# Second feed-forward of a four-layer graph network on Trainium2: work of four tiles of tokens interleaved, orders of the engines rewritten, scan stored in half the columns

## What is computed

```python
# 8 heads of 64; per graph: x is 256 tokens x 128
fx = x @ W_fx.T + b_fx;  xm = x @ W_x.T + b_x
sw = softmax((xm @ W_slice.T + b_slice) / temp)      # token -> 64 slices, per head
snorm = sw.sum(tokens)
st = einsum('bhnc,bhng->bhgc', fx, sw) / (snorm + 1e-5)   # 64 pooled tokens a graph, 512 wide
zxbcdt = st @ in_w.T                                 # z, x, B, C, dt forward and backward
dt = softplus(dt + dt_bias)
xBC = silu(causal_conv3(xBC))
y = scan(dt, exp(-dt*exp(A_log)), B, C, x)           # forward and backward over the 64 tokens
y = y + x * (x @ fcD_w.T + Dp)
yg = y * silu(z);  yg = yg * rsqrt(mean(yg**2) + 1e-5) * norm_w
ot = yg @ out_w.T
out = einsum('bhgc,bhng->bhnc', ot, sw) @ out_w.T + out_b
```

## Time and profile before

| what | value |
|---|---|
| median of three runs | 3244.88 us |
| profiled execution, from its first to its last instruction | 3243.7 us |
| TensorE busy in it | 2606.3 us, 80% |
| VectorE busy | 2274.7 us, 70% |
| ScalarE busy | 1783.4 us, 55% |
| GpSimd busy | 867.6 us, 27% |
| mean granted TensorE clock | 0.914 |
| this feed-forward | 1361 to 2071 us of the span |

### The profile page before, as it was taken

One profiled execution on the slowest core, in us unless ns is written; L12 is line 12 of the kernel. 1 busy time (PEld: TensorE's weight loads), 2 busy tenths in 40 slices (PEclk: granted clock), 3 DMA queues, 4 the chain that ended last, 5 costly groups with the idle time before them and its releaser, 6 DMA issues. The chain is left out here.

```text
span 3243.7 us, 68706 instructions
## 1 busy us (share of the span) xinstructions
PE 2606.3 (80%) x19386; PEld 2087.8 (64%) x19386; DVE 2274.7 (70%) x6679; ACT 1783.4 (55%) x5130; POOL 867.6 (27%) x863
## 2 busy tenths in 40 slices
PE   5899996992776941789999999699996888759992
PEld 4577776992675941656776777566664555549992
DVE  6777774666685656667777777499997688835555
ACT  2344434663674532755565555377774777726664
POOL 0233334663343432300000000000001155534442
PEclk9899997996887975989999999799998999969996
DMA  5111112334321213200000000000001000012225
GB/s 200 46 59 59 59 34 76 84 84 127 125 77 48 66 59 118 82 1 1 0 0 0 0 0 1 22 21 21 24 19 67 5 28 28 29 42 65 63 62 175
DMA packets 142548, 168.55 MB, mean 52 GB/s; under 512 B 19920, under 2 KB 118224, under 8 KB 141776
## 3 DMA queue, kind: packets, MB, share of 16 engines
q1 hardware_dynamic: 116688, 118.67, 12.1%
q0 software_dynamic: 21504, 44.74, 4.0%
q10 hardware_dynamic: 4224, 3.59, 0.4%
HBM read 115.87 MB, written 51.05 MB: 51 GB/s over the span
## 5 line engine op out<-in xcount | busy, mean ns | idle before, releaser
L1198 POOL DMA_INDIRECT y_rows<-ffn_e_rows_out,ffn_e_scatter_at x352 | 339.7, 965 | 385.7 <-DVE ffn_e_rows_out L1226 218.4
L1340 PE MATMUL bank<-ffn_e_xT,ffn_e_mine 128*128 128x128 f32 x3360 | 439.6, 278 | 2.2 <-ACT ffn_e_xT L1272 1.4
L1340 PEld LDWEIGHTS bank<-ffn_e_xT,ffn_e_mine 128*128 128x128 f32 x3360 | 410.4, 195 | 3.4 <-ACT ffn_e_xT L1272 2.2
L722 POOL DMA_INDIRECT sorted_rows<-ffn_rows,ffn_slot x320 | 315.5, 986 | 278.8 <-issue 266.4
L1274 ACT ACTIVATE ffn_e_mine<-constants 128x512 f32 (+1 forms) x352 | 250.2, 712 | 114.6 <-issue 65.3
L1246 DVE TENSOR_TENSOR ffn_e_hid<-ffn_e_act,bank 128x256 f32<-128x256 f32 (+1 forms) x280 | 136.1, 486 | 225.0 <-ACT ffn_e_act L1300 199.8
L1350 PE MATMUL bank<-ffn_e_mine,ffn_e_hid 128*128 128x128 f32 x1968 | 278.0, 276 | 2.6 <-DVE ffn_e_hid L1250 2.4
L2566 ACT ACTIVATE gnn_prob<-bank,gnn_low 128x256 f32<-128x256 f32 x512 | 203.5, 501 | 107.1 <-DVE gnn_low L2480 107.1
L1350 PEld LDWEIGHTS bank<-ffn_e_mine,ffn_e_hid 128*128 128x128 f32 x1968 | 247.5, 192 | 5.3 <-DVE ffn_e_hid L1250 4.8
L1300 ACT ACTIVATE ffn_e_act<-bank 128x256 f32<-128x256 f32 (+1 forms) x280 | 120.9, 432 | 106.0 <-PE bank L1340 104.9
L2480 DVE TENSOR_REDUCE gnn_low<-bank 128x2 f32<-128x512 f32 x256 | 159.0, 684 | 24.1 <-PE bank L2665 21.3
(11 more groups left out here) (505 smaller groups left out, 6583.6 us busy)
## 6 DMA issues: line engine op xcount, KB each, us to landing
g_adj<-in_adjT SPq DMA_DIRECT2D x48, 512.0 KB, 4.0
ffn_e_rows_in<-sorted_rows SPq DMA_DIRECT2D x346, 66.0 KB
ffn_c_y<-y_rows SPq DMA_DIRECT2D x80, 256.0 KB, 3.2
g_adj_rows<-in_adj SPq DMA_DIRECT2D x16, 512.0 KB, 4.3
gnn_adj<-in_adjT SPq DMA_DIRECT2D x16, 512.0 KB, 4.0
constants<-in_ffn SPq DMA_DIRECT2D x1, 6281.0 KB, 22.2
y_rows<-ffn_e_rows_out,ffn_e_scatter_at POOLq DMA_INDIRECT x352, 2.2
constants<-in_ffn SPq DMA_DIRECT2D x1, 5204.0 KB, 15.4
```

The lines of the kernel that those rows point to most:

```text
L722: eng.indirect_dma_start(c.sorted_rows, bass.IndirectOffsetOnAxis(r.slot[par][:, k, j:j + 1], 0), r.rows[par][:, j, :], None).then_inc(r.d ...
L1198: g.indirect_dma_start(c.y_rows, bass.IndirectOffsetOnAxis(scatter_at[par][:, k:k + 1], 0), rows_out[par][:, k, :], None).then_inc(scatter ...
L1340: ins = pe.matmul(chunk(part, ch), chunk(weights[:, i * HALF:(i + 1) * HALF], ch), x, start=True, stop=True)
```

## The change

`every_turn` is replaced for this stage by `staggered`, which writes turns -2 to 3 and 12 to 18 out and loops over 4 to 11. In one turn t the engines now do the logits of t+1, pooling and projections of t, scan of t-1, and outputs of t-2; X is updated for t-3. Every engine's `turn` is a new list in a new order, with the waits standing in it. To make room, sz, rsm and swT have two buffers, the projections use other banks, and `square` has a buffer of its own.

Three pieces of arithmetic are stored otherwise. Each head's scan matrix keeps only the block of the row's own graph, 64 columns instead of 128 (`own_masks`, `dt_run`, `dt_both`, `factor`, `decay`); the running sums become two 128x512 matmuls, the product with the tokens 16 matmuls of 64x64 weights. The sums over tokens ride in the unused half of the weights of the value matmuls (`value_w` has columns of ones), so L2294 is gone, and `pooled` does both graphs at once. dt is spread by VectorE alone.

```diff
+def staggered(eng, body, ahead, behind):
+
+    for t in range(-ahead, 4):
+        body(t, t % 2)
+    with eng.Fori(4, TURNS - 4, 2) as t:
+        body(t, 0)
+        body(t + 1, 1)
+    for t in range(TURNS - 4, TURNS + behind):
+        body(t, t % 2)
...
+                def turn(t, par):
+                    if on(t):
+                        after(g, g8_ready, t)
+                        after(g, xtok_ready, t)
+                        skip_term()
+                    if on(t - 1):
+                        add_bias(t - 1)
...
+                def pooled(t):
+
+                    low_half, high_half = slice(0, SL), slice(SL, P)
+                    v.tensor_scalar(sn[low_half], B[5][high_half, :], 1e-5, None, ALU.add)
+                    then(v, v.tensor_scalar(sn[high_half], B[4][low_half, :], 1e-5, None, ALU.add), stn, 2 * t + 1)
+                    then(v, v.reciprocal(sn[:], sn[:]), stn, 2 * t + 2)
...
+                def spread_dt():
+                    v.tensor_tensor(dt_run[:], dt[:].rearrange("p (d h) -> p d h", d=2)[:, :, :, None].broadcast_to([P, 2, HEADS2, SL]),
+                                    own_masks[:, :, None, :].broadcast_to([P, 2, HEADS2, SL]), ALU.mult).then_inc(dt_run_ready, 1)
...
+                def exp_dt():
+                    a.activation(e[:], m[:], ACT.Exp).then_inc(spe_ready, 1)
...
-                def pool_sums(t, g):
-                    pe.wait_ge(ph_ready, t * 2 + g + 1)
-                    mm(B[5 + 2 * g][:], ones[:], pooled_h[:, g, :], start=True, stop=True).then_inc(norm_ps, 1)
+                def pool_values():
+                    for a in range(2):
+                        for j in range(KC):
+                            cols = slice((2 * j + a) * SL, (2 * j + a + 1) * SL)
+                            ins = mm(B[5 - a][:, j * P:(j + 1) * P], value_w[:, a, j, :], pooled_h[:, :, cols], start=True, stop=True)
...
+                def running_sums():
+                    for d in range(2):
+                        ins = mm(B[3][:], masks[:, 1 - d, :], dt_run[:, d].rearrange("p h n -> p (h n)"), start=(d == 0), stop=(d == 1))
+                    ins.then_inc(D_ps, 1)
+
+                def product_y():
+                    for g in range(2):
+                        rows_ = slice(g * SL, (g + 1) * SL)
+                        for hd in range(HEADS2):
+                            cols = slice(hd * HD2, (hd + 1) * HD2)
+                            ins = mm(B[7][rows_, cols], decay[rows_, hd, :], xtok[rows_, cols], start=True, stop=True)
+                    ins.then_inc(y_ps, 1)
...
+                    if on(t + 1):
+                        after(pe, decay_ready, t - 1)
+                        lg_piece(1)
```

More of the change, by code:

```diff
@@ L46, in every_turn, with on, after @@
     body(count - 1, 1, False, True)
+def on(turn):
+    return not isinstance(turn, int) or 0 <= turn < TURNS
+def after(eng, sem, turn, each=1, nth=1):
+    if on(turn):
+        eng.wait_ge(sem, turn * each + nth)
+def staggered(eng, body, ahead, behind):
[6 more added lines that the diff above has]
+        body(t, t % 2)
 def every_four(eng, body):
@@ L1993, in pooled @@
[L1993 to L2007, removed]
+                    lg = heads(LG[k][:])
@@ L2106, in turn @@
-                    if not first:
-                        residual(t - 1)
-                    v.wait_ge(y_ps, t + 1)
-                    v.wait_ge(term_ready, t + 1)
-                    then(v, v.tensor_tensor(B[5][:], B[5][:], term[:], ALU.add), y_sum, t + 1)
-                    v.scalar_tensor_tensor(yg[:], B[5][:], 0.5, sz[:], ALU.mult, ALU.mult).then_inc(yg_ready, 1)
-                    if more:
-                        soft_b(t + 1, 1 - par, 3)
-                    v.wait_ge(ms_ready, t + 1)
@@ L2124, in _ @@
+                staggered(v, turn, AHEAD, BEHIND)
             @block.scalar
@@ L2225, in _ @@
+                staggered(a, turn, AHEAD, BEHIND)
             @block.tensor
@@ new lines, in tokens, with project_z, project_x @@
+                def tokens(ap):
+                    return ap.rearrange("p a s -> p (a s)")
+                def project_z():
+                    for k in range(KC):
+                        ins = mm(B[6][:], tokens(stT[:, k]), in_w[:, k, 0:IN2], start=(k == 0), stop=(k == KC - 1))
+                    ins.then_inc(z_ps, 1)
+                def project_x():
+                    for j in range(KC):
+                        for k in range(KC):
+                            ins = mm(B[5][:, j * P:(j + 1) * P], in_w[:, k, IN2 + j * P:IN2 + (j + 1) * P], tokens(stT[:, k]),
+                                     start=(k == 0), stop=(k == KC - 1))
+                    ins.then_inc(x_ps, 1)
@@ new lines, in project_bcd @@
+                def project_bcd():
+                    for k in range(KC):
+                        ins = mm(B[4][:, 2 * P:2 * P + 2 * HEADS2], tokens(stT[:, k]), in_w[:, k, 2 * IN2 + 2 * NS2:PROJ2],
+                                 start=(k == 0), stop=(k == KC - 1))
+                    for k in range(KC):
+                        ins = mm(B[4][:, 0:P], in_w[:, k, 2 * IN2:2 * IN2 + 2 * NS2], tokens(stT[:, k]), start=(k == 0), stop=(k == KC - 1))
+                    ins.then_inc(bcd_ps, 1)
@@ new lines, in tokens_T, with product_G @@
+                def tokens_T():
+                    for k in range(KC):
+                        ins = pe.transpose(B[3][:, k * P:(k + 1) * P], xT[:, k, :], c.ident[:])
+                    ins.then_inc(xt_ps, 1)
+                def product_G():
+                    for k in range(KC):
+                        mm(B[7][:, 2 * P:2 * P + HEADS2], xT[:, k, :], fcd[:, k, :], start=(k == 0), stop=(k == KC - 1))
+                    for d in range(2):
+                        for g in range(2):
+                            ins = mm(B[7][g * SL:(g + 1) * SL, d * SL:(d + 1) * SL], Bt[:, g * SL:(g + 1) * SL],
+                                     Cpad[:, 2 * d + g * SL:2 * d + (g + 1) * SL], start=True, stop=True)
+                    ins.then_inc(G_ps, 1)
@@ L2404 @@
+                staggered(pe, turn, AHEAD, BEHIND)
 HD_G, HD_A = 16, 32
```

632 lines of the change are left out of this document (337 added, 295 removed).

## The result

The changed kernel takes 3138.91 us (median of four runs, 3137.03 to 3141.17). The kernel before took 3244.14 us in four runs beside it (3239.91 to 3246.99). The ratio is 0.9676, with a 95% interval of 0.9662 to 0.969: 105.2 us less, where 84.5 were predicted.

What follows compares the result with a forecast made beforehand. TensorE was taken as the bound: 41.3 us a turn, less 2.4, 1.76 and 1.72, plus 0.5, 0.3 and 0.1, gave a 36.3 us period. With start and end, -84.5 us in all: 3160 us, range 3138 to 3192.

Steps and rivals of the forecast that it cites:

- the forecast case: Whole kernel: TensorE stays the bound, period 35.4 to 37.3 us, time 3148 to 3174 us; chance 0.66.
- case 2: Whole kernel: start and end cheaper and 64-column products cost less than now, 3135 to 3148 us; chance 0.04.
- start and end: Turns added by the four-turn stagger: start -3.8 and -16 us, turn 1 -8.3, end +15.7.
- The stops: TensorE's two standstills a turn, for ScalarE's swT copy and for yg before pooling, would go: -2.4 us a turn.
- The passes: TensorE's turn: running sums lose four passes, -1.76 us; sums over tokens leave, -1.72 us.
- The 64x64 products: TensorE's product with the tokens and small product of B and C: +0.5 us a turn taken for both.
- Case 4: Product with the tokens: a 64x64 pass doesn't overlap its load, costs 0.25 us, 3234 us (3203 at 0.18); chance 0.07.
- The two new waits: TensorE in the new turn: +0.3 us at logit 1 for decay, +0.1 us at the values for the pooled copy.
- the softmax of turn 0: Stage start: exps follow each other at about 2.5 us, three times -1.6, +1 for longer set-up: -3.8 us.
- the rest of turn 0: Turn 0 after its softmax: 31.9 us before; the scan leaves, about 16 us of copies, taps and softmax stay: -16 us.
- VectorE's ring: Rival: VectorE sets the period, 38.3 us up to 39.5, time 3188 to 3205 us; chance 0.18.
- The slower case: Softmax on VectorE: all four reciprocals wait 2.55 us for exps, VectorE needs 44.9 us a turn, 3280 us; chance 0.04.

## Why the prediction was right, and where its sizes were off

**What bounds it: right, and shown.** TensorE was the bound and still is: put-back passes cost all of their time, and its busy share is 100% of the steady part.

**The number: inside the range by luck.** The period of 34.63 lies outside the forecast case, 35.4 to 37.3, and 3138.91 us lies in case 2, 3135 to 3148, which was given 0.04. Nor did case 2 come as it was told: the small products were cheaper, but start and end were dearer. The steady turns gave 23.4 us more than reckoned and turn 1 gave 2.3 more; the start gave 7.1 less. Had the start come as reckoned, the time would be near 3132, below the range.

**The stops: right in kind, too small in size.** I read the two stops from the idle column, 1.18 and 1.25 us. That column counts from the modelled end of a matmul, which lies after the time at which the next one could have started. From start to start the same turn of before loses more:

```profile
1707.29 1.06 PE L2282 MATMUL bank<-constants,f_swT 128*128 128x128 f32 x8
1709.53 0.66 PE L2249 MATMUL bank<-ident,f_sw 128*128 128x128 f32 x4 [1.18 <-ACT f_swT L2145]
1710.02 1.06 PE L2282 MATMUL bank<-constants,f_swT 128*128 128x128 f32 x8
1710.91 0.60 PE L2363 MATMUL bank<-ident,f_xT 128*128 128x128 f32 x4
...
1716.95 1.06 PE L2282 MATMUL bank<-constants,f_swT 128*128 128x128 f32 x8
1718.11 1.97 PE L2387 MATMUL bank<-f_xtok,constants 128*128 128x64 f32 x16
```

Eight passes of L2282 cost 0.89 when nothing is in the way (1710.02 to 1710.91). In front of the waiting transpose they take 2.24, a stop of 1.35; in front of the product 1.16, a stop of 0.27 for decay that has no idle time in its row and that I missed. The transposes at 1719.92 take 1.86 for 0.44, a stop of 1.42. Together 3.04 us, not 2.43.

The low clock was missed too. In turns 2, 8 and 13 of before the eight passes of `pool_h` right behind the last stop took 5.2 us instead of 3.5; turn 8 stands in the earlier trace rows. The window's last three columns are granted clock, DMA share and GB/s:

```profile
1721.80:1725.20 3.40, 3.40 (x4) 1.37 (x5) 2.45 (x7) 0.98 (x3) 0.55 (x1) 0.52 0.00 0
1727.01 0.60 PE L2256 MATMUL bank<-ident,f_yn 128*128 128x128 f32 x4
```

From start to start that is 1727.01 - 1721.78 = 5.23 us, 1.7 too much, with a granted clock of 0.52 over most of it. The three turns lose 3 x 1.7 = 5.2 us so, and the changed kernel has none of it in its steady part. That its missing stops are the reason is not shown: the old order with the compact scan has such stops too and kept its full clock over the steady turns. It also makes the mean of before, 41.45, longer than the turn of 41.29. The prediction took its terms off 41.29 and compared the rest with 41.45, so 0.16 of its 5.15 us a turn, 2.2 us in all, had no term behind it.

**The passes: right.** The running sums went from 3.52 to 1.72, -1.80 for the -1.76 named. The ones-products are gone.

**The 64x64 products: taken too dear.** The term was +0.5; the product costs 1.83 for 1.81 and the one of B and C 0.37 for 0.64, together -0.25. The lower end of the bound was the truth and I stood a quarter of the way up. The rule of the Trainium skill, TensorE: Matmul & The Clock Gate, section LDWEIGHTS, that a weight load takes its columns over 1.2 GHz, gave an estimate of 1.7 us for the product, and the 0.057 us a pass agree. The drain that the Trainium skill, TensorEngine Tiling (Array Packing), section Key Properties, names at a change of tiling mode does not cost much: ahead of the product eight passes take 1712.90 - 1711.91 = 0.99 for 0.89, and behind it the logit takes 1715.69 - 1714.73 = 0.96 for 0.86, so 0.1 us at each change. Case 4's price of 0.25 us a pass came from no row.

**The two new waits: hardly there.** The +0.3 at logit 1 did not come: decay ends 6 us before it (1708.72 for 1714.73). The values cost 1732.41 - 1730.54 = 1.87 for twice 0.89, so 0.09 where +0.1 stood; that it is the wait is not shown. The block of VectorE by GpSimd came, and even on the sum too, and brought VectorE's busy time from the 29.1 us reckoned without it to 30.1; the new order had room for it, as the run with the bias late shows.

Summed again: 41.29 - 3.04 = 38.25; less 1.80 and 1.72, 34.73; less 0.25, 34.48; plus 0.2 at the changes of mode and 0.1 at the values, less 0.15 for transposes that run shorter between other neighbours, 34.6, for 34.63 measured. Of the 1.7 us by which the period was missed 0.6 are the stops, 0.75 the products, 0.3 the wait at logit 1 and 0.15 the transposes; the mode takes 0.2 back.

**Start and end,** by the starts of `pool_h`. Up to turn 1 the stage gained 70.1 - 57.4 = 12.7 us, not 19.8. Two steps failed. The first is the softmax of turn 0, where 3.8 were reckoned. Its last sw ends at 1387.12, for 1387.46 before, and the stage began 0.5 us earlier, so it gained nothing. The first exp starts 13.2 us into the stage for 10.8 before, 2.4 more where 1 was reckoned. And the exps of a piece follow those of the last at 2.3, 4.0 and 3.7 us, not at 2.5 each (4.08 before). The rows of the start show why: logit k+2 still waits for `soft_b` of k, and behind it come its lowest value and then the exps. One logit, two passes, takes 2.08 us there where 1.02 is its time at full clock, and it did so before as well. TensorE had stood still for 2.62 us before the first of them. The granted clock of the whole start is 0.79 in the window above.

```profile
1377.16 2.08 PE L2359 MATMUL bank<-f_logit_w,f_hT 128*128 128x512 f32 x2 [2.62 <-DVE f_sw L2027]
1380.86 2.08 PE L2359 MATMUL bank<-f_logit_w,f_hT 128*128 128x512 f32 x2 [1.62 <-DVE f_sw L2027]
...
1380.00 0.29 ACT L2225 ACTIVATE bank<-bank,f_low 128x64 f32<-128x64 f32 x1 [1.49 <-DVE f_low L2022]
1383.69 0.29 ACT L2225 ACTIVATE bank<-bank,f_low 128x64 f32<-128x64 f32 x1 [1.22 <-DVE f_low L2022]
```

The second is the rest of turn 0. From the last sw to turn 1 it takes 1417.92 - 1387.12 = 30.8 us, for 1431.07 - 1387.46 = 43.6 before: 12.8 less where 16 were reckoned. What holds the 3.2 us was not traced.

Turn 1 took 1448.65 - 1417.92 = 30.7 us for 41.3, -10.6 where -8.3 was said. Turns 2 to 15 gave 14 x -6.82 = -95.5 for -72.1. The end, from where turn 16 would begin (1448.65 + 14 x 34.63 = 1933.5) to the end of the last row below, 1966.7, takes 33.2 us for 18.0: +15.2 for +15.7. Sum: -12.7 - 10.6 - 95.5 + 15.2 = -103.6. VectorE's timeline of the end answers to the earlier trace rows; from the norm's end, 1952.9, the tail takes 13.8 us for 15.8 before, and the scan ahead of it 19.4 for the 17.9 reckoned.

```profile
1952.13 0.74 DVE L2128 SCALAR_TENSOR_TENSOR f_yn<-f_yg,f_rstdy,constants 128x512 f32<-128x512 f32 x1
...
1965.84 0.87 DVE L2044 BATCH_NORM_STATS2 ST<-X 128x6 f32<-128x128 f32 x4
```

**The signs.** Of those named, no stop at pooling, less than 0.6 at logit 1, the product within 1.8 to 2.8 and clock 1.00 came true. The period of 36 to 36.6 did not, 34.63, nor the end near 1986, 1966.7. VectorE's waits were half of what was said, 0.5 for the copy of x and 1.1 for the values, since its own work grew and the turn shrank. The rivals fell: VectorE's ring needs an extra 1.5 us before it shows, and the tiles were not dear but the reverse. The slower case rested on waits for the exps at each reciprocal. They are gone: VectorE's groups of the steady part show no idle time there, where it was 4.6 us a turn, and what is left is 1.1 us ahead of the lowest values. Whether another list would have brought them back was not tried.

```profile
L2026 DVE RECIPROCAL f_rsm<-f_sm 128x8 f32<-128x8 f32 x44 | 8.4, 191 | 0.0
```

## What to carry to other kernels

Where one engine bounds a stage, price its stops from start to start against the same group undisturbed elsewhere in the turn, not by the idle column, and look for stops in rows that show no idle time. Fewer passes pay only if the order leaves work to put over the chain that they covered: the compact scan brought 0.4 us a turn in the old order, while in the new one each of its four passes fewer is worth its full 0.43 us, 1.7 a turn. When two small matmuls can lie in opposite quarters of the array, alternate them.

## What the hardware showed that was not expected

- A 64x64 pass costs 0.057 us behind one in its own quarter and 0.034 behind one in the opposite quarter, the two graphs writing different partitions of one bank.
- The block between VectorE and GpSimd goes both ways. GpSimd's bias took 1.72 us beside the sum and the factor and 1.27 where it ran late, as before; VectorE's sum 1.45 and factor 1.16, where alone the factor takes 0.68.
- On chips where the whole kernel before took 8 to 9% longer the changed kernel's stage, which issues no DMA, took the same time within 1 us.
